# Queries and keys of the softmax: loaded from ScalarE's DMA queue in chunks of 16 l, instead of from SyncE's in chunks of 8

## The reference, cut to what matters

```python
B, N, E = 2, 64, 256;  H = 8;  d_k = 32
q  = (x_in @ Wq) ; k = (x_in @ Wk) ; v1 = (x_in @ Wv1) ; v2 = (x_in @ Wv2)      # [B, N, N, H, d_k]
scores = einsum('bilhd,bljhd->biljh', q, k) / sqrt(d_k)
att = softmax(scores, axis=2)                                                  # over l
out = einsum('biljh,bilhd,bljhd->bijhd', att, v1, v2)
h = layer_norm(x_in + out @ Wo); h = layer_norm(mlp(h) + h)
```

## Time and profile before

| what | value |
|---|---|
| median of 3 runs | 2487.22 us (2486.73 to 2491.69) |
| the profiled execution's own time | 2488.98 us |
| its span | 2487.2 us |
| mean granted TensorE clock | 0.970 |
| products (L330, first to last step) | about 262 to 1128 us |
| busy over the span | PE 86%, DVE 81%, ACT 52%, POOL 41% |

### The profile page before, as it was taken

How to read it: one execution, slowest core, us unless ns; L and a number is a source line. 1 busy time by engine, 2 the same in 40 slices (tenths; PEclk the granted TensorE clock), 3 DMA queues, 4 the chain that set the end, 5 groups by cost and what they waited for, 6 DMA issues and landing times. The chain is left out here.

```text
span 2487.2 us, 42555 instructions
## 1 busy us (share of the span) xinstructions
PE 2141.8 (86%) x16632; PEld 1396.7 (56%) x16632; DVE 2003.4 (81%) x2384; ACT 1298.0 (52%) x2834; POOL 1012.7 (41%) x513
## 2 busy tenths in 40 slices
PE   8999867776787676665999978999999999999998
PEld 7877412231232221113777756777777777777776
DVE  4426699979988999993877757888888888888886
ACT  3337467757756774541233334555555555555553
POOL 1103689979988999990110001111112111111111
PEclk9999889999999999997999998999999999999999
DMA  6668332124121212102233205232222223333332
GB/s 233 233 215 242 97 61 36 28 52 85 20 51 28 36 20 45 20 12 86 96 98 88 88 32 105 69 73 71 74 75 72 75 77 92 92 93 91 86 78 60
DMA packets 302504, 204.44 MB, mean 82 GB/s; under 512 B 202721, under 2 KB 280033, under 8 KB 297697
## 3 DMA queue, kind: packets, MB, share of 16 engines
q1 hardware_dynamic: 293600, 168.17, 27.4%
q0 software_dynamic: 8704, 33.56, 3.7%
HBM read 133.76 MB, written 67.90 MB: 81 GB/s over the span
## 5 line engine op out<-in xcount | busy, mean ns | idle before, releaser
L330 DVE TENSOR_TENSOR att_av<-att_att,att_v2ps 128x2816 f32<-128x2816 f32 (+2 forms) x288 | 775.5, 2749 | 59.5 <-PE att_bank L509 56.9
L330 POOL TENSOR_TENSOR att_av<-att_att,att_v2sb 128x1280 f32<-128x1280 f32 x256 | 744.6, 2936 | 73.7 <-PE att_bank L509 69.6
L509 PE MATMUL att_bank<-att_av,att_w 128*32 128x512 f32 x4096 | 546.9, 618 | 233.4 <-DVE att_av L330 190.2
L509 PEld LDWEIGHTS att_bank<-att_av,att_w 128*32 128x32 f32 x4096 | 136.7, 111 | 581.0 <-issue 283.4
L650 ACT ACTIVATE att_ev<-att_bank 128x512 f32<-128x512 f32 x512 | 297.3, 595 | 284.7 <-PE att_bank L509 215.3
L1693 DVE SCALAR_TENSOR_TENSOR mb_cv<-mb_bank,mb_cw,mb_cv 128x504 f32<-128x504 f32 (+2 forms) x480 | 342.7, 729 | 126.4 <-ACT mb_cv L1516 121.4
L1336 POOL TENSOR_TENSOR mb_rstd<-mb_ms,mb_neghalf 128x4 f32<-128x4 f32 x32 | 32.3, 1008 | 793.8 <-DVE mb_ms L1737 793.8
L1397 PE MATMUL mb_bank<-mb_xT_hi,dt_win_hi 128*128 128x512 f32 x576 | 242.1, 420 | 36.8 <-DVE mb_cv L1693 35.4
L1455 PE MATMUL mb_bank<-mb_wf,mb_y 128*128 128x256 f32 x1024 | 245.2, 387 | 0.8 <-DVE mb_y L1733 0.8
L1397 PE MATMUL mb_bank<-mb_xT_lo,dt_win_hi 128*128 128x512 f32 x576 | 229.2, 398 | 0.0
L1397 PE MATMUL mb_bank<-mb_xT_hi,dt_win_lo 128*128 128x512 f32 x576 | 228.8, 397 | 0.0
(11 more groups left out here) (182 smaller groups left out, 3331.6 us busy)
## 6 DMA issues: line engine op xcount, KB each, us to landing
att_xin<-in_x SPq DMA_DIRECT2D x32, 512.0 KB, 4.4
qk_t<-att_qk POOLq DMA_DIRECT2D x16, 1024.0 KB, 5.1
v<-att_vs POOLq DMA_DIRECT2D x16, 1024.0 KB, 5.2
mixed_t<-att_ev SPq DMA_DIRECT2D x1024, 8.0 KB
mb_dAb<-dA_rows SPq DMA_DIRECT2D x32, 512.0 KB, 5.6
mb_dAb<-dA_cols SPq DMA_DIRECT2D x32, 512.0 KB, 6.2
att_q<-qk_t SPq DMA_DIRECT2D x8, 1024.0 KB, 9.9
att_kb<-qk_t SPq DMA_DIRECT2D x128, 64.0 KB, 2.0
```

Of the source, the lines that this page charges most:

```text
L330: return eng.tensor_tensor(av[t % 2][:, :, d0:d1, :], a.unsqueeze(2).broadcast_to((P, 2, d1 - d0, N)), v2.unsqueeze(1).broadcast_to((P, 2, ...
L509: mm = pe.matmul(bank[r % NB][s * M:(s + 1) * M, :], w[i // WB % 2][:, i % WB, s, :], av[r // 2 % 2][:, i % 2, s * STRIP_D:(s + 1) * STRIP ...
```

## The change

`load_q` and `load_k` move from SP's program into ACT's, and `KL` goes from 8 to 16: 4 chunks a pair instead of 8, each with 4 DMAs of 128 KB instead of 64 KB; `kb` doubles in size. Chunks 2 and 3 are issued by `copy_scores` behind the copy of the last group of chunks 0 and 1 (g = 3 and 7). The queries and chunks 0 and 1 (`load_first`, 2 + 8 DMAs) of pair 0 are issued at v = 0 behind `xT_hi(XN + 1)`, after a wait for all stores of q and k; of pair 1 at v = 6; of pairs 2 and 3 at the end of step m = 20 of pairs 0 and 1. SP's program keeps the loads of x, v1 and v2 and the stores, in the same order.

```diff
-    KL = 8
+    KL = 16
@@ sync
-            def load_q(n): ...
-            def load_k(n, c): ...
-            sp.wait_ge(kb_zeroed, 2)
-            for u in range(2):
-                sp.wait_ge(qk_stored[u], XN // 2 * 16)
-            load_q(0)
-            load_k(0, 0)
-            load_k(0, 1)
-            for v in (4, 5, 6):
-                load_x(XN + v)
-            load_k(0, 2)
...
-            for v in range(11, 15):
+            for v in range(4, 15):
                 load_x(XN + v)
@@ products, per chunk c and store e
-                    if c % 2 == 0 and n < PAIRS:
-                        for k in {0: (2, 3), 1: (4, 5), 2: (6,), 3: (7,)}.get(e, ()):
-                            load_k(n, k)
                     store(c, e)
...
-                    if c % 2 == 0 and n + 1 < PAIRS and e == 9:
-                        load_q(n + 1)
-                        load_k(n + 1, 0)
-                        load_k(n + 1, 1)
@@ scalar
             act.wait_ge(w_zeroed, 2)
+            act.wait_ge(kb_zeroed, 2)
+            def load_q(n): ...        # as before, on act
+            def load_k(n, c): ...     # as before, on act
@@ copy_scores(n, g)
+                c = g * LB // KL
+                if g * LB % KL == KL - LB and c < 2:
+                    load_k(n, c + 2)
+            def load_first(n):
+                load_q(n)
+                load_k(n, 0)
+                load_k(n, 1)
@@ strips v, behind xT_hi(XN + v + 1)
+                if v == 0:
+                    for u in range(2):
+                        act.wait_ge(qk_stored[u], XN // 2 * 16)
+                    load_first(0)
+                if v == 6:
+                    load_first(1)
@@ steps, behind exps(n, *EXPS[m])
+                if n + 1 < PAIRS and m == 20:
+                    load_first(n + 1)
```

More of the change, by code:

```diff
@@ L227, in load_x @@
                     sp.dma_start(xin[u % NX][:, :, :], x_rows[u % XN]).then_inc(x_loaded[u % NX], 16)
[L229 to L243, removed]
             def load_v2(c):
@@ L302, in _ @@
             for c in range(NC):
-                n = c // 2 + 1
                 if c + 1 < NC:
@@ L585, in _, with load_q, load_k @@
             act.wait_ge(w_zeroed, 2)
+            act.wait_ge(kb_zeroed, 2)
+            def load_q(n):
+                need(act, scored, n * NG)
+                for b in range(B):
+                    act.dma_start(q[b * 64:(b + 1) * 64, :],
+                                 qk_dram[n * 64:(n + 1) * 64, b * N * N:(b + 1) * N * N]).then_inc(q_loaded, 16)
+            def load_k(n, c):
+                need(act, scored, n * NG + (c - 1) * (KL // LB))
+                for b in range(B):
+                    for h2 in range(2):
+                        lo = (2 * b + h2) * DK
+                        src = qk_dram[E + n * 64 + h2 * DK:E + n * 64 + (h2 + 1) * DK,
+                                      b * N * N + c * KL * N:b * N * N + (c + 1) * KL * N]
+                        act.dma_start(kb[c % 2][lo:lo + DK, h2, :, :], src.rearrange("p (l j) -> p l j", l=KL))\
+                            .then_inc(k_loaded[c % 2], 16)
             def copy_scores(n, g):
```

## The result

The changed kernel takes 2469.41 us (median of 4 runs, 2469.16 to 2475.43) against 2488.03 us of the kernel before on the same chip (4 runs). The ratio is 0.9929, with a 95% interval of 0.991 to 0.9947. The profiled execution took 2475.43 us with a span of 2473.6.

The account below looks back on a forecast made before the run. DVE was taken to bound the products, its idle time there being waits for PE's rows. The terms -26 + 7 + 0 + 0 - 1.6 + 1 + 0.9 gave -18.7 us, so 2469 us, range 2452 to 2489.

Parts of the forecast that it names:

- Part 1: Products, steps with scores: taking the key loads off SP's queue gains 26 us, bounds -29 and -15.
- part 2: Products: issuing later key chunks of pairs 1 to 3 on ACT's queue costs 7 us, bounds 0 and +20.
- part 3: Products, step 20: queries and first key chunks of pairs 2 and 3 on ACT, 0 us net, bounds -9 and +10.
- Part 4: The v strips: 0 us at v = 0, -1.6 us at v = 6, +1 us for chunks 2 and 3 of pair 0.
- Part 5: The start: doubled memsets of `kb` delay those of `w`, for which ACT waits, +0.9 us.
- A: ACT's issues, sharing the issue path with SP's stores, cost more than SP's: 2480.5 us, chance 0.20.
- B: At each `load_first`, a full queue holds ACT behind the queries: 25 us on the forecast, 2493.5 us, chance 0.12.
- C: Products: gaps under scores come from PE's own chain, not SP, so only -10 instead of -26: 2484.5 us, chance 0.11.
- D: Products: ACT hides its issues wholly and the step-20 loads bring a gain: about -33, 2454 us, chance 0.12.
- DVE's waits: Sign in the products: DVE's waits for PE fall from 56.9 to about 35 us.
- the end of the products: Sign: the products end near 1110 us instead of 1128.
- SP's free time: Sign in the products: SP's wait for evictions grows well over 113 us.

Follow-up runs that it names:

- e2: The changed kernel with key chunks of 8 l instead of 16, still on ACT's queue: 2466.12 us.
- e11: The changed kernel with bare waits for score groups put into SP's program before stores 0 to 3 of chunks with scores, no DMA added: 2478.64 us.
- e10: The kernel before with only the places of the key loads among SP's first stores of a pair moved: 2480.93 us.
- e7: The changed kernel with the query loads of pairs 2 and 3 moving only 64 of 4096 columns, that computation left out: 2457.54 us.
- e6: The changed kernel with queries and first two key chunks of pairs 2 and 3 issued one DMA a step in steps 11 to 22: 2459.15 us.
- e3: The changed kernel with queries and first two key chunks of pairs 2 and 3 issued by SP again, behind store 9: 2467.88 us.
- e4: The changed kernel with key chunks 2 and 3 of pairs 1 to 3 issued by SP again, before stores 1 and 2: 2468.81 us.
- e5: The changed kernel with the ten first issues of pairs 2 and 3 at step 11 instead of 20: 2470.31 us.

## Why the prediction was right, and where it was not

**The total and its place: right, with luck in it.** 2469 was forecast, 2469.41 came, and the gain is in the products. But the parts don't agree term by term. Parts 1 and 2 gave 26.2 us in the steps with scores where 19 were forecast, and the other steps, for which part 3 had 0, are 7.2 us longer. That these two cancel was not foreseen.

**Part 1 and 2 (keys, -26 and +7): place right, reason half right.** Steps 0 to 12 of the three pairs are 26.2 us shorter. That is the -26, but with the cost of part 2 already in it, so the bursts on ACT cost about nothing, not 7; e2 says the same with three times as many of them. ACT's issue was 0.44 us, about the 0.42 assumed. The reason given for part 1 was the time of SP's issues, and SP's "only long wait" was said to be the one for evictions. SP also waited 15.0 us for PE in `load_k`, which the reader could have seen in the waits of its queue. e11 shows that waits in SP's program, without any issue, give back up to half of the gain (9.2 of 18.6 us, with 21.9 us of waiting); e10 shows that removing that wait alone is not enough, because the keys then come late. The share of the issues themselves stays open. The windows of the earlier trace rows were said to hold about 38 steps; DVE's 101.51 us of busy time are 33, the number that the 12 us rest on.

**Part 3 (queries, 0): right in size, by two errors that cancel.** DVE's two gaps were 9.0 us and are 9.2 (3.98 + 5.18). The sum had a pause of 5.3 us, 2 to 3 us for a late store, and 3 us absorbed. The pause is 5.6 us of issues, but ACT's wait for the late store was 5.0 and 4.5 us, and more than 3 us was absorbed: in e7 a pause of 6.2 us leaves DVE no gap over 1.4 us. e7 shows that the late store is the part that counts, and e6 that it can be had back. Part 3 also did not see the small waits that make up the 7.2 us of the other steps, 1.5 of it in the last pair, which has no queries to load at all (DVE waits for ACT's exponentials 3.4 us in all, 1.4 before); what makes the rest was not looked for, and it may be in part the difference between two executions.

**Part 4 (v strips): small and off.** At v = 0 PE got its first scores at 137.12 instead of 135.72, +1.4 where I had 0. Its wait there shrank from 5.96 to 2.53 us, as foreseen, but behind the pause of ACT it had begun later:

```profile
119.81 1.14 ACTq L546 DMA_DIRECT2D att_q<-qk_t  x2
120.98 4.63 ACTq L556 DMA_DIRECT2D att_kb<-qk_t  x8
125.66 1.09 ACT L656 ACTIVATE att_vs<-att_bank 128x512 f32<-128x512 f32 x2 [6.31 <-issue]
```

```profile
137.12 1.90 PE L440 MATMUL att_x<-att_kb,att_q 64*64 64x128 f32 x16 [2.53 <-issue]
```

At v = 6 ACT's wait of 6.91 us for the store of v is gone, and one of 3.23 us stands at 207.63. Up to the first product the whole difference is +1.3 us (262.37 against 261.12), where parts 4 and 5 had +0.3. This can't be told from nothing: e3, e4, e5, e6, e7 and e11 have the changed kernel's program up to there, and their first products start between 259.35 and 264.34.

**Part 5 (start, +0.9): wrong and small.** The memsets did double (3.54 us), but ACT's table load began at 6.23 instead of 5.97, ahead of the end of the memsets of `w` at 6.75, so they did not set its start. PE's first projection began at 9.90 instead of 9.88: it waited for DVE, which split the weights until about 8.5 us in both.

**Rivals.** A did not happen: 443 ns against 422, with SP's stores at 567 ns in the median as before. The 21 ns are not from the doubled bytes, for the loads of 64 KB on ACT in e2 read 443 ns too; and ACT's longest issue, 1.66 us, is below SP's longest before, 2.60. The Trainium skill ("Perfetto Trace Analysis", section "DMA Instruction — HWDGE (DVE, Sync)") says that the block that makes descriptors is shared by the sequencers of DVE and Sync; it does not name ACT's, and these rows neither show nor exclude that ACT's waits for it too. B did not happen: 8 loads went out behind the 2 MB in 4.13 us. C was wrong: the large gaps under scores did go. D was half there, in that ACT hid the issues of the keys wholly; a gain in part 3 came only with e6.

**The signs announced.** DVE's waits (35 said, 34.9 found), the end of the products (1110, 1107) and SP's free time were right; ACT's waits for stores fell to 40.3 us and not to 30: 9.5 of it are behind the queries and the other 31, in ten places, mostly in the first steps of a chunk, where v2 is loaded.

## What to carry to other kernels

In a DMA queue that carries stores, look for loads that wait on a semaphore ahead of a finished store. Their wait counts beside their issue (up to 9 us here), and moving them back can starve the reader (e10). More slack for each load (a larger chunk) or another queue cured both here, and either alone was enough. Loads of megabytes in one piece made small stores late whether SP or ACT issued them (e3 and the changed kernel are alike), and cutting them in pieces spread over the steps gave 10 us (e6). And compare stages by the same steps, not by windows of time.

## What the runs showed of the hardware

An issue on ACT goes out while earlier work of the engine still stands: the first query load at 338.31 lies inside the `build` that ends at 338.7, and the exponentials that the program has ahead of it start only at 338.74. Large loads on ACT's queue delay 8 KB stores on SP's: with the 3 MB under way a store made ACT wait 4.5 to 6.6 us (changed kernel, e5); with 1 MB of keys (e7) no store was late behind them.

A stall costs more than its own length, since TensorE's granted clock fell during it. In the kernel before, PE stood 4.85 us for ACT until 297.74; from 297.7 to 303 the mean granted clock is 0.53, that is for the most part the lower of its two levels (1.2 GHz), and 32 matmuls of scores took 3.44 us where 2.07 is usual (278.34):

```profile
278.34 2.07 PE L485 MATMUL att_x<-att_kb,att_q 64*64 64x128 f32 x32
...
297.74 1.94 PE L509 MATMUL att_bank<-att_av,att_w 128*32 128x512 f32 x8 [4.85 <-ACT att_ev L650]
299.61 3.44 PE L485 MATMUL att_x<-att_kb,att_q 64*64 64x128 f32 x32
```

In the first stretch of scores the mean clock is 0.89 before and 0.96 now. How much of the 26.2 us this is was not tried apart. And the landing of a 128 KB load of keys was 8.4 us in the median in the changed kernel (where half follow 2 MB of queries at once) and 3.2 us in e6 (a quarter):

```profile
att_kb<-qk_t ACTq DMA_DIRECT2D x64, 128.0 KB, 8.4
```

```profile
att_kb<-qk_t ACTq DMA_DIRECT2D x64, 128.0 KB, 3.2
```
